# Output scatters held on GpSimd until batch 1's sorted rows are loaded

## The chip, the core and the metric

The kernel runs on one core of a Trainium2 chip. TensorE multiplies and transposes, VectorE and ScalarE move and transform tiles, GpSimd here adds constants early on and later issues the scatters, and SP issues plain DMAs. The metric is the device time of one execution in microseconds.

## What is computed

Two transformer layers over x of shape 2 x 512 x 128 (two batches of 512 tokens): attention against 77 keys, a feed-forward with low-rank experts, attention again, and at last a feed-forward that sends each token to one of 8 experts. Only the last part matters here:

```python
t = x.reshape(-1, d)                       # normalised rows
route_prob = softmax(t @ switch_w + switch_b)
routes = argmax(route_prob, axis=-1)
for e in range(8):
    h = gelu(t @ w1[e] + b1[e])            # 128 -> 512
    y = h @ w2[e] + b2[e]                  # 512 -> 128
    out = where(routes == e, y, out)
out = out * route_prob_max                 # and x + out is the result
```

## The kernel before

The last part sorts the rows by expert, each batch for itself. A batch has 4 tiles of 128 tokens, and its sorted rows fill at most 11 tiles (NSB), since each expert begins a new tile; both batches have NS = 22 tiles, 0 to 10 for batch 0 and 11 to 21 for batch 1. The way of a batch is:

- VectorE works out a slot for each row (`rank`, L809 to L823) and its probability (`prob`).
- GpSimd scatters the rows with their normalised form, probability and token number from ROW to the DRAM tensor `slots`: four indirect DMAs a batch (L514), each of which adds 16 to `rows_sent[b]`.
- SP waits for these four and loads the sorted rows back into XS in four pieces (L433): tiles 0, 1 to 2, 3 to 5 and 6 to 10 of the batch (LOADS). Each piece has its own semaphore `slots_in[b][i]`.
- For each tile t, TensorE transposes XS (L1079), ScalarE copies the expert's first weights (L621) and the transpose (L623), TensorE makes the first product (L1086), VectorE adds the bias (L846), ScalarE applies gelu (L628), TensorE makes the second product (L1097), and VectorE adds the bias (L855, YB) and scales and adds the residual into XS (L856, which signals `z_ready`). The first product of tile t stands in TensorE's list right ahead of the second product of tile t - 2.
- GpSimd scatters XS[:, t, 0:D] into the output by token number (L520), 22 indirect DMAs in the order of t, each behind `z_ready`. Its last wait is for all of them (`stored`, L523).

Each engine runs its own list of instructions in the order of one table (`schedule`). On GpSimd the four row scatters of batch 0 come first, then those of batch 1, then the 22 output scatters. TensorE waits for a piece of the load before it transposes the first tile of it (L1076), and VectorE once a piece for the token numbers (L852). No other engine waits for the output scatters, and XS has room for all 22 tiles, so no tile's place is used twice.

Of the kernel before, what the change touches and what calls it, by code (L numbers as in the profile page):

```python
# [30 lines left out]
B = 2  # L31
# [31 lines left out]
LOADS = [(0, 1), (1, 3), (3, 6), (6, NSB)]  # L63
# [127 lines left out]
def build(nc, x, ctx3, att0, att1, consts, small, rows, ffn0w, loraB, sw, w1, b1, w2, b2, empty, out):  # L191
# [9 lines left out]
    with stages:  # L201
# [3 lines left out]
        def sem(name):  # L205
            return stages.enter_context(nc.semaphore(name))
# [138 lines left out]
        slots_in = [[sem(f"slots_in{b}_{i}") for i in range(len(LOADS))] for b in range(B)]  # L345
# [61 lines left out]
        @block.sync  # L407
        def _(sp):
            xv = x.rearrange("(b t p) d -> b p t d", b=B, p=128)
            sp.dma_start(X[:, 0], xv[0]).then_inc(in_x[0], 16)  # L410
            sp.dma_start(ATT[0][:, 0:A_Q], att0[:, 0:A_Q]).then_inc(in_wk, 16)
            sp.dma_start(ATT[0][:, A_Q:], att0[:, A_Q:]).then_inc(in_att[0], 16)
            sp.dma_start(X[:, 1], xv[1]).then_inc(in_x[1], 16)
            sp.dma_start(ROWS[:, :], rows.partition_broadcast(128)).then_inc(in_rows, 16)
            sp.dma_start(W0[:, :], ffn0w).then_inc(in_w0, 16)
            for i in range(3):
                sp.dma_start(LB[32 * i:32 * i + 32, :], loraB).then_inc(in_lb, 16)
            sp.dma_start(ATT[1][:, :], att1).then_inc(in_att[1], 16)
            sp.dma_start(SW[:, :], sw).then_inc(in_moe, 16)
            sp.dma_start(B1[:, :], b1).then_inc(in_moe, 16)  # L420
            sp.dma_start(B2[:, :], b2.partition_broadcast(128)).then_inc(in_moe, 16)
            for e in range(E):
                sp.dma_start(W1[:, e * F:(e + 1) * F], w1[:, e]).then_inc(in_w1[e], 16)
                sp.dma_start(W2[:, e * NF * D:(e + 1) * NF * D], w2[:, e]).then_inc(in_w2[e], 16)
            sv = slots.rearrange("(t p) w -> p t w", p=128)
            flat = "(p t) w -> p (t w)"
            sp.dma_start(slots.rearrange(flat, p=128), empty.rearrange(flat, p=128)).then_inc(preset, 16)
            for b in range(B):

                sp.wait_ge(rows_sent[b], 16 * NQ)  # L430
                for i, (t0, t1) in enumerate(LOADS):
                    t0, t1 = b * NSB + t0, b * NSB + t1
                    sp.dma_start(XS[:, t0:t1], sv[:, t0:t1]).then_inc(slots_in[b][i], 16)  # L433

        @block.gpsimd
        def _(pool):
            counts = {}

            def finish(ins, signal):

                counts[signal.name] = counts.get(signal.name, 0) + 1
                ins.then_inc(signal, 1)
                pool.wait_ge(signal, counts[signal.name])

            finish(pool.memset(eps[:, :], EPS), zeroed)

            finish(pool.memset(KG[:, :, 0::2, GK:GP].bitcast(F32), 0.0), zeroed)
            finish(pool.memset(KG[:, :, 1::2, 0:PAD].bitcast(F32), 0.0), zeroed)
            finish(pool.memset(MR[:, :, :, :, :], 0.0), zeroed)
            finish(pool.memset(MR[:, :, :, :, 0:2], 1.0), zeroed)  # L450
            finish(pool.memset(VP[:, :, :, :, :, HALF * VC:], 0.0), zeroed)
            pool.wait_ge(in_small, 16)
            finish(pool.tensor_scalar(tau8[:, :], SMALL[:, S_TAU:S_TAU + B], RS8, None, ALU.mult), tau_ready)
            r = slice(ONES, KR)
            sel = [SMALL[r, S_SEL + i:S_SEL + i + 1] for i in range(3)]
            finish(pool.tensor_scalar(dscaled[r, :], SMALL[r, S_DEL:S_DEL + B * KEYS], RS8, None, ALU.mult), delta_part)
            finish(pool.tensor_copy(dhigh[r, :], dscaled[r, :]), delta_part)
            finish(pool.tensor_tensor(dlow[r, :], dscaled[r, :], dhigh[r, :].bitcast(F32), ALU.subtract), delta_part)

            finish(pool.tensor_scalar(dscaled[r, :], dlow[r, :], sel[1], sel[2], ALU.mult, ALU.subtract), delta_part)  # L460
            finish(pool.tensor_scalar(dlow[r, :], dhigh[r, :].bitcast(F32), sel[0], None, ALU.mult), delta_part)
            low = dlow[r, :].unsqueeze(1).to_broadcast([KR - ONES, G, B * KEYS])
            rest = dscaled[r, :].unsqueeze(1).to_broadcast([KR - ONES, G, B * KEYS])
            finish(pool.tensor_tensor(Ks[r].rearrange("p g b k -> p g (b k)"), low, rest, ALU.add), delta_ready)
            pool.wait_ge(in_con, 16)

            vm = CON[0:TW, C_VM:C_VM + NT * HALF].rearrange("p (j h) -> p j h", j=NT)
            def ones_columns(l, b):
                for half in range(2):
                    o = VP[:, l, b, :, half, 0:HALF * VC].rearrange("p j (h c) -> p j h c", c=VC)[:, :, :, DK]  # L470
                    finish(pool.tensor_copy(o, vm), ones_col)

            def moe_constants():
                tail = CON[:, C_TAIL:C_TAIL + 4 * TILES].rearrange("p (t c) -> p t c", c=4)
                finish(pool.tensor_copy(ROW[:, :, 2 * D:RW], tail), rows_set)
                finish(pool.tensor_copy(trib[:, :], CON[:, C_TRI:C_TRI + 128]), binary)
                finish(pool.memset(onesb[:, :], 1.0), binary)

            finish(pool.memset(mhalf[:, :], -0.5), powers)
            for s in steps:  # L480
                if s[0] == "ln" and s[1] == 3:
                    b = s[2]
                    pool.wait_ge(var_ready, b + 1)
                    pool.tensor_tensor(rstd[:, b], var_eps[:, b], mhalf[:, :], ALU.pow).then_inc(rstd3_ready, 1)
                if s[0] == "vp" and s[3] == 0:
                    ones_columns(s[1], s[2])
                if s == ("km", 1, 0):
                    moe_constants()
                if s[0] == "km" and s != ("km", 0, 0):
                    _, l, b = s  # L490
                    pool.wait_ge(k_split, B * l + b + 1)
                    pool.wait_ge(delta_ready, 1)
                    if l == 1:

                        pool.wait_ge(scores_ready, 2 * NT * (b + 1))
                    for odd in (0, 1):
                        finish(pool.tensor_tensor(*masked_k(b, odd), ALU.mult), kg_pool)  # L497
                elif s[0] == "xt" and s[1] < 3:

                    _, st, b = s  # L500
                    c = (R_BO0, R_WOB, R_BO1)[st]
                    if s == ("xt", 0, 0):
                        pool.wait_ge(in_rows, 16)
                    pool.wait_ge(xn_ready, (nth["xn", st, b] + 1) * NQ)
                    row = ROWS[:, c:c + D].unsqueeze(1).to_broadcast([128, NQ, D])
                    finish(pool.tensor_tensor(X[:, b], X[:, b], row, ALU.add), pre_added)  # L506
                elif s[0] == "rank":

                    b = s[1]
                    pool.wait_ge(preset, 16)  # L510
                    pool.wait_ge(slot_ready, b + 1)
                    pool.wait_ge(p_ready, b + 1)
                    for i in range(b * NQ, (b + 1) * NQ):
                        pool.indirect_dma_start(slots, bass.IndirectOffsetOnAxis(ap=slot[:, i:i + 1], axis=0), ROW[:, i], None,  # L514
                                                bounds_check=NS * 128 - 1, oob_is_err=False).then_inc(rows_sent[b], 16)
                elif s[0] == "moe" and s[1] >= 2:

                    t = s[1] - 2
                    pool.wait_ge(z_ready, t + 1)
                    pool.indirect_dma_start(out, bass.IndirectOffsetOnAxis(ap=token[:, t:t + 1], axis=0), XS[:, t, 0:D], None,  # L520
                                            bounds_check=B * S - 1, oob_is_err=False).then_inc(stored, 16)

            pool.wait_ge(stored, 16 * NS)  # L523

        @block.scalar
        def _(act):
# [7 lines left out]
            for s in steps:  # L534
                kind = s[0]
                if kind == "ln":

                    _, st, b = s
                    if st == 3:
                        continue  # L540
# [659 lines left out]
```

## Time and profile before

| | |
|---|---|
| median of 3 runs | 209.26 us (208.22 to 212.48) |
| the profiled execution | 207.62 us |
| its span | 205.7 us |
| mean granted clock of TensorE | 0.934 |
| TensorE busy | 170.5 us (83%) |
| VectorE busy | 134.2 us (65%) |
| ScalarE busy | 88.4 us (43%) |
| GpSimd busy | 59.5 us (29%) |

The span is what lies between the first and the last instruction of the profiled execution; times in rows are microseconds from its start. A busy engine is not by that alone the one that sets the time: the chain of waits tells which work ended last at each step. A granted clock of 1.00 is 2.4 GHz and 0.50 is 1.2 GHz.

### The profile page before, as it was taken

Reading aid. Unit: us, or ns where it says so; the run is one execution under the profiler, and the core shown is the slowest. Engines: PE = TensorE matmul, PEld = TensorE weight load, DVE = VectorE, ACT = ScalarE, POOL = GpSimd, SP = SyncE. Lnnn points to the kernel's source line nnn. Section 1 sums busy time; section 2 is a strip of 40 time slices with the busy share of each in tenths; the row PEclk is TensorE's granted clock in tenths of the full one; section 3 lists DMA queues with packets and bytes.
Section 4 is the critical chain, followed back from the end, with each engine's and each line's share of the span. In section 5 each row is a group of like instructions: output and inputs, shape, how many; then the busy total and the mean of one; then the engine's idle time right before and its main releaser. Section 6 shows DMA issues by size and latency. Waiting matters only on the chain.

```text
span 205.7 us, 3632 instructions
## 1 busy us (share of the span) xinstructions
PE 170.5 (83%) x1141; PEld 143.6 (70%) x1141; DVE 134.2 (65%) x388; ACT 88.4 (43%) x170; POOL 59.5 (29%) x73
## 2 busy tenths in 40 slices
PE   7556999989999967698999998952878599999960
PEld 2315888979958944574986778851868599999950
DVE  6889987589653778983347966454386266666750
ACT  2270268334542353322258163341354357677710
POOL 8992030000405160100020002054006454545551
PEclk9965599999999999999999999999679969999996
DMA  5999970000000000000000000012801560000000
GB/s 200 290 356 407 506 304 3 0 0 3 2 0 3 0 0 0 2 3 0 0 0 0 3 0 0 0 55 86 254 0 65 141 192 21 29 9 4 21 24 2
DMA packets 9218, 15.36 MB, mean 75 GB/s; under 512 B 1578, under 2 KB 6069, under 8 KB 9136
## 3 DMA queue, kind: packets, MB, share of 16 engines
q1 hardware_dynamic: 7680, 13.00, 18.3%
q0 software_dynamic: 1088, 1.60, 2.4%
q10 hardware_dynamic: 432, 0.53, 0.7%
q8 instruction: 10, 0.16, 0.3%
q14 instruction: 8, 0.07, 0.1%
HBM read 13.53 MB, written 5.44 MB: 92 GB/s over the span
## 4 chain that ended last, share of the span: by engine, by line
PE 56%; DVE 26%; issue 8%; ACT 5%; POOL 2%; DVEq 1%; ACTq 0%; another core or an unknown queue 0%; POOLq 0%
PE acc L985 12%; PE scores L1086 8%; PE acc L1097 7%; PE shared L941 5%; DVE QG L711 4%; PE scores L966 4%; PE shared L1042 4%; PE shared L1028 3%; PE shared L916 2%; PE shared L895 2%; PE shared L923 2%; DVE stats L652 2%; DVE QG L643 2%; DVE XN L670 2%; PE shared L1002 2%
## 5 line engine op out<-in xcount | busy, mean ns | idle before, releaser
L985 PE MATMUL acc<-VP,P 123*128 123x128 f32 (+1 forms) x320 | 41.8, 276 | 0.6 <-ACT P L588 0.6
L985 PEld LDWEIGHTS acc<-VP,P 123*128 123x128 f32 (+1 forms) x320 | 39.8, 191 | 2.8 <-issue 1.3
L588 ACT ACTIVATE P<-scores 123x512 f32<-123x512 f32 (+1 forms) x40 | 22.9, 595 | 27.0 <-PE scores L966 24.2
L1086 PE MATMUL scores<-XST,HT 128*128 128x128 f32 x176 | 26.3, 297 | 3.3 <-ACT XST L623 3.3
L721 DVE TENSOR_REDUCE MR<-shared 128x4 f32<-128x308 f32 x64 | 26.9, 469 | 2.2 <-PE shared L941 2.0
L520 POOL DMA_INDIRECT out<-XS,token x22 | 21.3, 969 | 20.3 <-DVE XS L856 18.3
L506 POOL TENSOR_TENSOR X<-X,ROWS 128x512 f32<-128x512 f32 x6 | 7.7, 1278 | 66.8 <-DVE XN L670 66.7
L1086 PEld LDWEIGHTS scores<-XST,HT 128*128 128x128 f32 x176 | 23.7, 209 | 4.4 <-ACT XST L623 4.3
L941 PE MATMUL shared<-KG,QG 98*128 98x308 f32 x64 | 21.3, 389 | 6.1 <-DVE QG L711 2.9
L846 DVE TENSOR_TENSOR HT<-scores,B 128x512 f32<-128x512 f32 x22 | 15.2, 691 | 16.3 <-PE scores L1086 13.1
L1097 PE MATMUL acc<-W,HT 128*128 x176 | 24.5, 286 | 0.2 <-DVE XS L856 0.2
L1097 PEld LDWEIGHTS acc<-W,HT 128*128 128x128 f32 x176 | 22.8, 203 | 0.4 <-issue 0.4
L628 ACT ACTIVATE HT<-HT 128x512 f32<-128x512 f32 x22 | 13.9, 630 | 17.9 <-DVE HT L846 10.0
L966 PE MATMUL scores<-QG,KG 102*123 102x512 f32 (+1 forms) x48 | 19.7, 458 | 1.7 <-issue 1.6
L941 PEld LDWEIGHTS shared<-KG,QG 98*128 98x128 f32 x64 | 12.7, 213 | 11.3 <-issue 5.2
L711 DVE SCALAR_TENSOR_TENSOR QG<-shared,ATT,QG 32x512 fp32r<-32x512 f32 x16 | 11.9, 745 | 6.1 <-ACT QG L575 5.8
L514 POOL DMA_INDIRECT slots<-ROW,slot x8 | 8.1, 1015 | 21.8 <-DVE ROW L789 11.4
L621 ACT ACTIVATE HT<-W 128x512 f32 x22 | 13.8, 629 | 1.2 <-issue 0.9
L575 ACT ACTIVATE QG<-shared,ATT 64x512 fp32r<-64x512 f32 x16 | 10.9, 684 | 5.4 <-PE shared L923 5.2
L580 ACT ACTIVATE QG<-shared 6x512 fp32r<-6x512 f32 x8 | 4.7, 585 | 17.7 <-PE shared L950 17.6
L966 PEld LDWEIGHTS scores<-QG,KG 102*123 102x123 f32 (+1 forms) x48 | 8.4, 191 | 3.5 <-issue 2.5
L497 POOL TENSOR_TENSOR KG<-Ks,CON 102x616 fp32r<-102x616 f32 x6 | 7.5, 1249 | 10.4 <-DVE Ks L685 10.0
(122 smaller groups left out, 248.4 us busy)
## 6 DMA issues: line engine op xcount, KB each, us to landing
W<-in_w SPq DMA_DIRECT2D x16, 256.0 KB, 8.5
slots<-in_empty SPq DMA_DIRECT2D x1, 2860.0 KB, 15.9
XS<-slots SPq DMA_DIRECT2D x2, 650.0 KB, 6.0
XS<-slots SPq DMA_DIRECT2D x2, 390.0 KB, 4.6
W<-in_ffn0w SPq DMA_DIRECT2D x1, 534.0 KB, 8.3
XS<-slots SPq DMA_DIRECT2D x2, 260.0 KB, 3.0
X<-in_x SPq DMA_DIRECT2D x2, 256.0 KB, 4.3
B<-in_b SPq DMA_DIRECT2D x1, 512.0 KB, 7.3
```

Source lines behind the costliest of these rows:

```text
L520: pool.indirect_dma_start(out, bass.IndirectOffsetOnAxis(ap=token[:, t:t + 1], axis=0), XS[:, t, 0:D], None, bounds_check=B * S - 1, oob_i ...
L588: act.activation(P[0:w, n % NP], scores[n % 2][0:w, :], ACT.Exp).then_inc(probs_ready, 1)
L621: act.activation(W1C[:, n % 2], W1[:, bass.ds(expert * F, F)], ACT.Identity).then_inc(w1_ready, 1)
L628: act.activation(HG1[:, t % NHB], HB[:, t % 2], ACT.Gelu_apprx_tanh).then_inc(gelu_ready, 1)
L711: dve.scalar_tensor_tensor(QG[64:96, b, g], bank(s)[64 * odd:64 * odd + 32, :], ATT[l][0:32, A_BQ + g:A_BQ + g + 1], QG[0:32, b, g].bitcas ...
L721: dve.tensor_reduce(MR[:, b, qt, g, 2:2 + HG], bank(s)[:, 0:GK].rearrange("p (h k) -> p h k", h=HG), AX.X, ALU.max).then_inc(max_read, 1)
L846: dve.tensor_tensor(HB[:, t % 2].rearrange("p (k n) -> p k n", k=NF), hidden[t % 2][:, :].rearrange("p (k n) -> p k n", k=NF), bias, ALU.a ...
L941: pe.matmul(bank(s)[:, 0:GK], QG[0:ONES + 2, b, g, 128 * qt:128 * qt + 128], KG[0:ONES + 2, b, g, off:off + GK], start=True, stop=True).th ...
L966: ins = pe.matmul(scores[n % 2][0:w, :], KG[:, b, g, c:c + w], QG[:, b, g], start=(i == 0), stop=(i == len(parts) - 1))
L985: ins = pe.matmul(acc[qt // 2][:, c:c + VW], P[0:w, n % NP, 128 * qt:128 * qt + 128], VP[0:w, l, b, j, half], start=(t == 0 and qt % 2 == ...
L1086: ins = pe.matmul(hidden[t % 2][:, 128 * k:128 * (k + 1)], W1C[:, t % 2, 128 * k:128 * (k + 1)], XST[:, t % 2], start=True, stop=True)
L1097: ins = pe.matmul(acc[n % 2][:, 0:D], HG1[:, n % NHB, 128 * k:128 * (k + 1)], W2[:, bass.ds(expert[n] * (NF * D) + D * k, D)], start=(k == ...
```

## The change

Ahead of the scatter of tile 0 GpSimd now waits for the four pieces of batch 1's load.

```diff
@@ -516,6 +516,9 @@
                 elif s[0] == "moe" and s[1] >= 2:
 
                     t = s[1] - 2
+                    if t == 0:
+                        for i in range(len(LOADS)):
+                            pool.wait_ge(slots_in[B - 1][i], 16)
                     pool.wait_ge(z_ready, t + 1)
                     pool.indirect_dma_start(out, bass.IndirectOffsetOnAxis(ap=token[:, t:t + 1], axis=0), XS[:, t, 0:D], None,
                                             bounds_check=B * S - 1, oob_is_err=False).then_inc(stored, 16)
```

On GpSimd, at the end of its list, with the semaphores that each instruction waits for (`slots_in1_0` to `slots_in1_3` are the four pieces of batch 1; L523 is the scatter's line in the changed file, L520 before):

```order
 L514 DMA slots<-ROW,slot 2816x260 [waits p_ready,slot_ready,preset]
 L514 DMA slots<-ROW,slot 2816x260 x3
-L520 DMA out<-XS,token 1024x128 [waits z_ready] x22
+L523 DMA out<-XS,token 1024x128 [waits slots_in1_3,slots_in1_2,z_ready,slots_in1_1,slots_in1_0]
+L523 DMA out<-XS,token 1024x128 [waits z_ready] x21
 L201 UNCONDITIONAL_BRANCH [waits stored]
```

No instruction changes its place, on this engine or another; the first of the 22 output scatters has four more waits.

## Rows read from the trace of the kernel before

**Rows 1.** Part 4 of the page: shares of the chain of waits by engine.

```profile
PE 56%; DVE 26%; issue 8%; ACT 5%; POOL 2%; DVEq 1%; ACTq 0%; another core or an unknown queue 0%; POOLq 0%
```

**Rows 2.** Chain in order of time: start us, us, what.

```profile
191.05 0.89 PE scores L1086 x8
191.94 0.89 PE acc L1097 x8
192.83 0.11 PE shared L1079
...
200.71 0.97 POOL out L520
```

**Rows 3.** Timeline of GpSimd: start us, us, engine, line, operation [idle before it]

```profile
155.18 1.04 POOL L514 DMA_INDIRECT slots<-ROW,slot  x1 [11.38 <-DVE ROW L789]
...
160.35 0.97 POOL L520 DMA_INDIRECT out<-XS,token  x1 [0.30 <-issue]
161.62 0.97 POOL L520 DMA_INDIRECT out<-XS,token  x1 [0.30 <-issue]
165.41 0.97 POOL L520 DMA_INDIRECT out<-XS,token  x1 [2.81 <-DVE XS L856]
...
171.47 0.97 POOL L520 DMA_INDIRECT out<-XS,token  x1 [1.54 <-DVE XS L856]
...
181.16 0.97 POOL L520 DMA_INDIRECT out<-XS,token  x1 [1.13 <-DVE XS L856]
...
190.66 0.97 POOL L520 DMA_INDIRECT out<-XS,token  x1 [0.93 <-DVE XS L856]
...
198.13 0.97 POOL L520 DMA_INDIRECT out<-XS,token  x1 [0.82 <-DVE XS L856]
199.41 1.00 POOL L520 DMA_INDIRECT out<-XS,token  x1 [0.30 <-issue]
200.71 0.97 POOL L520 DMA_INDIRECT out<-XS,token  x1 [0.30 <-issue]
```

**Rows 4.** The load queue's timeline: the last of batch 1's four loads.

```profile
162.97 0.49 SPq L433 DMA_DIRECT2D XS<-slots  x1
```

**Rows 5.** Part 6 of the page: issues of this kind, KB each, median us to landing.

```profile
XS<-slots SPq DMA_DIRECT2D x2, 650.0 KB, 6.0
```

**Rows 6.** Windows: PE, PEld, DVE, ACT, POOL busy, PEclk, DMA share, GB/s.

```profile
165.00:166.00 1.00, 1.00 (x7) 1.00 (x6) 0.92 (x3) 0.19 (x1) 0.59 (x1) 0.50 1.06 293
...
168.00:169.00 1.00, 1.00 (x9) 1.00 (x9) 0.17 (x1) 0.98 (x3) 0.22 (x2) 0.81 0.17 47
169.00:170.00 1.00, 1.00 (x11) 1.00 (x10) 0.69 (x1) 0.24 (x2) 0.94 (x1) 1.00 0.00 0
```

**Rows 7.** TensorE: line L1079's waits (us, times), then its timeline.

```profile
  DMA XS<-slots: 8.1, 2
...
164.19 1.40 PE L1086 MATMUL scores<-XST,HT 128*128 128x128 f32 x8 [2.12 <-ACT XST L623]
...
173.48 0.27 PE L1079 MATMUL shared<-CON,XS 128*128 128x128 f32 x1
```

**Rows 8.** Timeline of VectorE, columns as for GpSimd.

```profile
157.70 0.69 DVE L846 TENSOR_TENSOR HT<-scores,B 128x512 f32<-128x512 f32 x1 [0.63 <-ACT HT L628]
...
161.69 0.69 DVE L846 TENSOR_TENSOR HT<-scores,B 128x512 f32<-128x512 f32 x1 [2.65 <-PE scores L1086]
...
164.26 0.35 DVE L856 SCALAR_TENSOR_TENSOR XS<-YB,XS 128x128 f32<-128x128 f32 x1
165.09 0.69 DVE L846 TENSOR_TENSOR HT<-scores,B 128x512 f32<-128x512 f32 x1 [0.47 <-issue]
...
172.22 0.35 DVE L856 SCALAR_TENSOR_TENSOR XS<-YB,XS 128x128 f32<-128x128 f32 x1
173.04 0.69 DVE L846 TENSOR_TENSOR HT<-scores,B 128x512 f32<-128x512 f32 x1 [0.46 <-PE scores L1086]
```

**Rows 9.** Line L856 as a whole: ns min/median/max, first and last start.

```profile
L856 DVE SCALAR_TENSOR_TENSOR XS<-YB,XS x22: 350/352/353, 156.7 to 199.2; 128x128 f32<-128x128 f32 x22
```

## The prediction

> **What bounds the kernel now.** I read the shares of the chain of waits first, then the chain in order of time at its end, then the timelines of the four engines and of the load queue through the last 50 us. By the shares, TensorE carries 56% of the path and GpSimd 2% [rows 1]. In the stretch that the change touches, the path is TensorE's: it is one tile after another there, first product 0.89 us, second product 0.89 us, a transpose 0.11 us, which is 1.90 us a tile. Only behind the last product does the chain leave TensorE, for VectorE's last additions and then GpSimd, whose last three scatters start at 198.13, 199.41 and 200.71 [rows 2, 3]. So GpSimd counts at the very end only. What the reader is to see: a scatter before that end is late for nobody, because the kernel has no wait on `stored` but GpSimd's own at the end, and XS[:, t] is neither loaded nor written again after the scatter of tile t.
>
> The profiled execution took 207.62 us, with a span of 205.7 us, so 1.9 us lie around the span. The median of the three runs shown is 209.26 us. I make the sum as a difference on the span and add it to the median.
>
> **What the change adds.** Four waits on constants in GpSimd's queue ahead of the scatter of tile 0, and nothing else. They are queue instructions without data: I put them at nothing; what separates two scatters that wait for nothing, 0.30 us [rows 3], bounds one of them from above, and all four lie under the hold or within the slack below.
>
> *How long is the hold?* Of batch 1's four loads SP issues the last and largest (tiles 17 to 21, 650 KB) at 162.97 [rows 4]; such a load lands 6.0 us after its issue [rows 5]. That puts the release at R = 162.97 + 6.0 = 169.0 us. The DMA share agrees: 1.06 from 165 to 166, 0.17 from 168 to 169, and 0.00 after [rows 6]. Before, tile 0's scatter ran at 160.35 right behind the four row scatters of batch 1, so the hold is real. It moves the scatters of tiles 0 to 4, the first five of the queue, behind R.
>
> *What queues up behind it?* All 22 output scatters stand behind the waiting one, and nothing else does: batch 1's row scatters stand ahead of it in the queue and are the work on which the loads depend, so there is no circle. The first scatter starts about 0.8 us after its release, as tile 2's did (its VectorE operation ends at 164.26 + 0.35 = 164.61, the scatter starts at 165.41). Back to back the scatters start 1.29 us apart: 155.18 to 161.62 holds five intervals (four row scatters, then tiles 0 and 1), 1.29 each, and 198.13 to 200.71 two, 1.29 each [rows 3, 8]. Tile k is then scattered at 169.8 + 1.29 k, as long as that is later than before. Before, they came 1.90 apart. Tile 5: 176.3 against 171.47. Tile 10: 182.7 against 181.16. Tile 15: 189.2 against 190.66. The lag of 1.5 us at tile 10 shrinks by 1.90 - 1.29 = 0.61 a tile, so it is gone at tile 13, eight tiles before the end. If it were not, the last scatter could start at 169.8 + 21 x 1.29 = 196.9; it waits for its tile and starts at 200.71 as before. **Slack 3.8 us, cost 0.**
>
> *What leaves the load window?* The DMA work of the scatters that started before R, five of them, three at 160.35, 161.62 and 165.41. If batch 1's loads get faster by that, nobody gains: over all 22 transposes TensorE's waits for a load are two records of the first one, the matmul's and its weight load's, 8.1 us together. Tile 11, the first of batch 1, is transposed at 173.48 without such a wait [rows 7]; even the last load is there 4.5 us before it. Gain 0. The bound is zero on both sides unless something else hangs on the scatters, which the rivals price.
>
> **A rule that speaks against the change.** The backlog makes GpSimd denser: 0.97 us of issuing in each 1.29 instead of in each 1.90, from 169.8 to about 187 us. VectorE's last operation of a tile reads two SBUF tensors, and it already runs into a scatter now: the one at 172.22 lies within the scatter of 171.47 to 172.44, and takes 0.35 us like the others. Its 22 instances span 350 to 353 ns, overlapped or not [rows 3, 8, 9]. So I charge nothing.
>
> The Trainium skill, page "SBUF — State Buffer", section "SBUF: two separate sides", says that VectorE and GpSimd share a pair of ports under an exclusive lock, and that a VectorE operation with two SBUF inputs against a GpSimd operation that reads SBUF leaves the second one fully blocked. By that page the scatter issue would hold such an operation up; the 353 ns maximum in this trace does not agree for this pair.
>
> **The sum.** Waits 0, backlog 0 (3.8 us of slack), loads 0, port 0: span 205.7, median 209.3 us.
>
> **Rivals.**
> *1. No change in time* (the forecast), 0.80, 209.3 us.
>
> *2. The early scatters disturb the other engines, and holding them gives that back.* There is something to explain. VectorE's bias operation of tile 4 starts at 161.69, 3.99 us after the one at 157.70, and the next at 165.09, 3.40 us later [rows 8]. Against a period of 1.90 that is 2.1 + 1.5 = 3.6 us lost. TensorE sits idle for 2.12 us until 164.19 [rows 7], and its granted clock is then 0.50 (1.2 GHz) from 165 to 166 and back at 1.00 at 169 [rows 6]; VectorE's bias operations take 7.95 us from 165.09 to 173.04, four tiles, against 7.6, another 0.35. For it: the scatters of 160.35 and 161.62 lie inside. Against it: tile 4's operation was due at 157.70 + 1.90 = 159.6, before the first output scatter started, so the first part has another cause; and the same scatters at the same density do no harm from 198 us on. If only the second part goes, 1.5 + 0.35: 209.26 - 1.9 = 207.4 us. If all of it goes, 3.95: 205.3 us. Chance 0.12, of which a third for all of it; where the stall comes differently in every execution, this moves the median either way by as much.
>
> *3. GpSimd becomes the bound at the end: slower.* The place is the scatter queue behind R. It decides from R + 0.8 + 21 x 1.29 > 200.71, that is from R = 172.8 on, or at R = 169.0 from a spacing of (200.71 - 169.8) / 21 = 1.47 us instead of 1.29. Each microsecond of R beyond it costs one. Over 2% needs R = 177.0 or a spacing of 1.67. Against it: both loads of this size took 6.0 us as a median, and the spacing is measured. For it: thirteen scatters in a row are not in the trace, six are. With a spacing of 1.6 us: 200.71 becomes 203.4, and the time 212.0 us. Chance 0.05.
>
> *4. The dense scatters hold VectorE up after all: slower.* VectorE works 0.69 + 0.35 us in its two longest operations of a tile [rows 8]; with the third, the addition of YB on half the columns of the first and so at most 0.35, that is 1.39 us in each 1.90, so it decides once the hindrance exceeds some 0.5 us a tile; a full scatter of 0.97 would cost 0.46 on each of the nine tiles that pass between 169.8 and 187 us, 4.1 us: 213.4 us. Against it stand the 353 ns. Chance 0.03.
>
> **The numbers.** The forecast is 209.3 us. The three runs of before lie from 1.0 below to 3.2 above their median, so a median of the changed kernel may lie a microsecond or two off with no cause in the change. Low end: the smaller gain of rival 2 (207.4) less about that 1.0, 206.5. High end: the middle plus two thirds of the upper scatter, 211.5; that leaves rivals 3 and 4 and the larger case of rival 2 outside, with the tails about 2 in 10. Over 2% (4.2 us, about what a measurement of this kernel can tell from no change) faster needs all of rival 2 and a little luck: 0.05. Over 2% slower: rival 4, a bad case of rival 3, or a median drawn from the upper end of such runs: 0.06. The rest is 0.89.
>
> **What would show it.** Right: GpSimd's first output scatter starts at about 169.8 and the following ones 1.28 to 1.30 apart up to about tile 13, then 1.90 apart; the last starts at the same distance from the end of the span as now, 205.7 - 200.7 = 5.0 us; TensorE's tiles keep 1.90; L856 keeps 0.35. Wrong in a step: a first scatter after 173 (the load estimate), a spacing over 1.47 (the catch-up), L856 or L846 longer (the port), or a span whose stretch from 157 to 169 us is shorter by 2 us or more (rival 2). The forecast falls if the stall near 160 us goes with the scatters and does not come back when they do.

## The result, and the profile after

| | before | changed |
|---|---|---|
| median | 209.24 us (6 runs, 208.22 to 212.48) | 215.42 us (6 runs, 213.34 to 215.91) |
| the profiled execution | 207.62 us | 214.13 us |
| its span | 205.7 us | 212.2 us |

The changed kernel took 1.027 times as long, with a 95% interval of 1.0227 to 1.0313. The forecast was 209.3 us, no change. It stands wrong for this pair. In the same comparison in later runs, on three chips, the ratio lay between 0.9987 and 1.0015, and the kernel before took 204.8 us on each of the five chips met in later runs. (The record does not name the chip that ran the pair, so it may have been a sixth chip or one of the five at another time.) So there are two things to explain, and the document keeps them apart: the pair of the record, and what the change does in the later runs.

The page of the changed kernel, busy times, then the slices of TensorE and its clock, and the chain's shares by engine. (Lines of the changed file stand three higher than those of before: L849 is the bias operation, L1089 the first product, L523 the output scatter.)

```profile
PE 173.3 (82%) x1141; PEld 146.2 (69%) x1141; DVE 134.6 (63%) x388; ACT 88.7 (42%) x170; POOL 59.6 (28%) x73
...
PE   7745999989999976779999998636997991799960
...
PEclk9996799999999999999999999975569999699996
...
PE 50%; DVE 28%; issue 8%; another core or an unknown queue 4%; ACT 4%; POOL 2%; DVEq 2%; ACTq 0%; POOLq 0%
```

Busy times have hardly moved, GpSimd still has 2% of the path, and 4% of it are now put down to "an unknown queue", where [rows 1] had 0%. TensorE has a hole near four fifths of the span. GpSimd's timeline shows the hold and what follows:

```profile
160.34 0.97 POOL L514 DMA_INDIRECT slots<-ROW,slot  x1 [0.30 <-issue]
170.97 1.04 POOL L523 DMA_INDIRECT out<-XS,token  x1 [9.66 <-DMA XS<-slots]
172.31 0.97 POOL L523 DMA_INDIRECT out<-XS,token  x1 [0.30 <-issue]
...
179.96 0.97 POOL L523 DMA_INDIRECT out<-XS,token  x1 [0.30 <-issue]
182.56 0.97 POOL L523 DMA_INDIRECT out<-XS,token  x1 [1.64 <-DVE XS L859]
...
207.22 0.97 POOL L523 DMA_INDIRECT out<-XS,token  x1 [0.30 <-issue]
```

The first output scatter comes at 170.97 and not at 160.35 [rows 3]; eight of them start 1.27 to 1.34 us apart; and at the ninth it is GpSimd that waits for VectorE. So the queue of scatters had caught up by tile 8, and was not what made the kernel later. VectorE's bias operations were late instead:

```profile
158.97 0.69 DVE L849 TENSOR_TENSOR HT<-scores,B 128x512 f32<-128x512 f32 x1 [0.64 <-ACT HT L631]
...
162.28 0.69 DVE L849 TENSOR_TENSOR HT<-scores,B 128x512 f32<-128x512 f32 x1 [1.97 <-remote]
...
171.63 0.69 DVE L849 TENSOR_TENSOR HT<-scores,B 128x512 f32<-128x512 f32 x1 [0.46 <-PE scores L1089]
...
176.81 0.69 DVE L849 TENSOR_TENSOR HT<-scores,B 128x512 f32<-128x512 f32 x1 [3.74 <-remote]
183.34 0.69 DVE L849 TENSOR_TENSOR HT<-scores,B 128x512 f32<-128x512 f32 x1 [1.57 <-remote]
185.59 0.69 DVE L849 TENSOR_TENSOR HT<-scores,B 128x512 f32<-128x512 f32 x1 [0.82 <-issue]
```

The steps of tiles 9 to 10 to 11 are 5.2 and 6.5 us, where 1.90 is the rule. Two more operations that wait for TensorE alone start late there: VectorE's addition behind the second product of tile 8, and ScalarE's copy of the transpose of tile 12.

```profile
181.09 0.29 DVE L858 TENSOR_TENSOR YB<-acc,B 128x128 f32<-128x128 f32 x1 [3.59 <-remote]
```

```profile
181.01 0.28 ACT L626 ACTIVATE XST<-shared 128x128 f32<-128x128 f32 x1 [2.16 <-remote]
```

TensorE's own rows in that stretch (L1100 is the second product, L1082 the transpose; those of 173.07 and 173.97 belong to tiles 8 and 12):

```profile
170.28 1.06 PE L1089 MATMUL scores<-XST,HT 128*128 128x128 f32 x8
...
172.18 1.06 PE L1089 MATMUL scores<-XST,HT 128*128 128x128 f32 x8
173.07 1.06 PE L1100 MATMUL acc<-W,HT 128*128 x8
173.97 0.27 PE L1082 MATMUL shared<-CON,XS 128*128 128x128 f32 x1
174.08 1.06 PE L1089 MATMUL scores<-XST,HT 128*128 128x128 f32 x8
...
181.35 2.04 PE L1089 MATMUL scores<-XST,HT 128*128 128x128 f32 x8 [5.21 <-ACT XST L626]
```

The product of tile 10 stands in the trace from 172.18 to 173.24, and VectorE, which waits for nothing else, begins on it at 176.81: 3.6 us later, and "remote" means that no recorded work ended then. Further down TensorE's list the lateness is larger: the second product of tile 8 ends in the record at 174.13 and is taken up at 181.09 (7.0 us), the transpose of tile 12 at 174.24 and 181.01 (6.8 us), tile 11's first product at 175.14 and 183.34 (8.2 us). ScalarE sees it as VectorE does, so the cause does not lie in VectorE alone. Tile 9's product, still undisturbed, ended at 170.28 + 1.06 = 171.34 and was taken up at 171.63, 0.3 us later. Either TensorE's work was really late and its record is not (the ends of matmuls are modelled), or its signals were; these rows do not tell which. I call it the late signals. TensorE itself then idles 5.21 us, until ScalarE's late copy for tile 12 is there, and its granted clock falls from 1.00 to 0.50. Windows of 2 us, columns as in [rows 6]:

```profile
174.00:176.00 2.00, 2.00 (x20) 1.90 (x18) 0.00 (x0) 0.00 (x0) 1.52 (x2) 1.00 0.02 1
176.00:178.00 2.00, 0.14 (x2) 0.00 (x0) 0.69 (x1) 0.47 (x1) 1.56 (x2) 1.00 0.08 19
178.00:180.00 2.00, 0.00 (x0) 0.00 (x0) 0.00 (x0) 0.79 (x2) 1.39 (x3) 1.00 0.10 33
180.00:182.00 2.00, 0.65 (x3) 0.66 (x4) 0.64 (x2) 0.28 (x1) 0.93 (x1) 0.85 0.14 46
182.00:184.00 2.00, 2.00 (x11) 2.00 (x11) 0.66 (x1) 0.00 (x0) 0.97 (x1) 0.50 0.00 0
```

DMA is nearly idle there, and GpSimd alone keeps its pace. The kernel before has the same thing on a smaller scale. The first product of tile 4 and the second of tile 2 end in the record at 159.11 and 160.00, and VectorE takes them up at 161.69 [rows 8] and 163.94, 2.6 and 3.9 us later; ScalarE's copy at 163.86 is 3.8 us behind its transpose.

```profile
157.95 1.16 PE L1086 MATMUL scores<-XST,HT 128*128 128x128 f32 x8 [0.68 <-ACT XST L623]
158.94 1.06 PE L1097 MATMUL acc<-W,HT 128*128 x8
```

```profile
163.94 0.29 DVE L855 TENSOR_TENSOR YB<-acc,B 128x128 f32<-128x128 f32 x1 [1.55 <-remote]
```

**Where the 6.5 us of span went.** From the bias operation of tile 3 to that of tile 21 the trace of before has 157.70 to 195.77, 38.1 us, the changed one 158.97 to 202.28, 43.3 us, and behind that both have 9.9 us. So 5.2 us lie in the tiles 3 to 21, and 1.3 us had been lost before tile 3, ahead of anything that the change touches. An undisturbed trace (below) has 34.0 us for the same 18 steps: before lost 4.0 us in the record pair, the changed kernel 9.3, each with the lower clock behind the late signals.

The 5.2 us are a difference of two things. From tile 3 to tile 9 the kernel before takes 157.70 to 173.04, 15.3 us [rows 8], the changed one 158.97 to 171.63, 12.7 us, and the undisturbed trace 11.3: the stall near 160 us has shrunk from 4.0 to 1.4 us, a gain of 2.7. From tile 9 to tile 12 the changed kernel takes 171.63 to 185.59, 14.0 us, where the other two take 6.0: a loss of 7.9 behind the hold. From there on all three are alike. Each figure is from one execution.

### The profile page after: what moved, and what is told of

It reads as the page before. It is cut to its first block, busy times and chain, and to the rows that moved or that the text cites. A ratio compares the mean times of both kernels' runs of the same rounds, so it can differ in the third digit from the quotient of the medians.

```text
span 212.2 us, 3634 instructions
## 1 busy us (share of the span) xinstructions
PE 173.3 (82%) x1141; PEld 146.2 (69%) x1141; DVE 134.6 (63%) x388; ACT 88.7 (42%) x170; POOL 59.6 (28%) x73
## 4 chain that ended last, share of the span: by engine, by line
PE 50%; DVE 28%; issue 8%; another core or an unknown queue 4%; ACT 4%; POOL 2%; DVEq 2%; ACTq 0%; POOLq 0%
PE acc L988 11%; PE scores L1089 6%; PE shared L944 5%; PE acc L1100 4%; DVE QG L714 4%; PE shared L1045 4%; PE scores L969 4%; DVE HT L849 2%; PE shared L1031 2%; PE shared L898 2%; PE shared L919 2%; PE shared L926 2%; DVE stats L655 2%; PE shared L1018 2%
## 5 line engine op out<-in xcount | busy, mean ns | idle before, releaser
L1089 PE MATMUL scores<-XST,HT 128*128 128x128 f32 x176 | 27.9, 309 | 7.3 <-ACT XST L626 7.1
L1089 PEld LDWEIGHTS scores<-XST,HT 128*128 128x128 f32 x176 | 25.2, 221 | 8.8 <-ACT XST L626 8.4
L523 POOL DMA_INDIRECT out<-XS,token x22 | 21.4, 972 | 25.5 <-DVE XS L859 13.1
L849 DVE TENSOR_TENSOR HT<-scores,B 128x512 f32<-128x512 f32 x22 | 15.2, 692 | 19.8 <-PE scores L1089 9.4
L944 PE MATMUL shared<-KG,QG 98*128 98x308 f32 x64 | 20.8, 381 | 7.7 <-DVE QG L714 7.2
L1100 PE MATMUL acc<-W,HT 128*128 x176 | 24.8, 288 | 0.2 <-DVE XS L859 0.2
L1100 PEld LDWEIGHTS acc<-W,HT 128*128 128x128 f32 x176 | 23.0, 205 | 0.4 <-issue 0.4
```

The source lines that it names most:

```text
L849: dve.tensor_tensor(HB[:, t % 2].rearrange("p (k n) -> p k n", k=NF), hidden[t % 2][:, :].rearrange("p (k n) -> p k n", k=NF), bias, ALU.a ...
L944: pe.matmul(bank(s)[:, 0:GK], QG[0:ONES + 2, b, g, 128 * qt:128 * qt + 128], KG[0:ONES + 2, b, g, off:off + GK], start=True, stop=True).th ...
L1089: ins = pe.matmul(hidden[t % 2][:, 128 * k:128 * (k + 1)], W1C[:, t % 2, 128 * k:128 * (k + 1)], XST[:, t % 2], start=True, stop=True)
L1100: ins = pe.matmul(acc[n % 2][:, 0:D], HG1[:, n % NHB, 128 * k:128 * (k + 1)], W2[:, bass.ds(expert[n] * (NF * D) + D * k, D)], start=(k == ...
```

## The experiments

Each was compared with the kernel before, run beside it on the same chip. "This chip" is below the chip of the run in question. I began with the nearest theory: a dense run of scatters (1.28 us apart) makes TensorE's signals late. For it spoke that all work of TensorE that was taken up late, in both traces, ends in the record while such a run is going on: at 159.11 and 160.00 in the run of scatters that start from 155.18 to 161.62 [rows 3], and in the changed kernel at 160.38 (tile 4, taken up 1.9 us late) in that from 156.45 to 160.34, and from 173.24 to 175.14 in that from 170.97 to 179.96. Against it spoke that batch 0's four row scatters, from 135.47 on in the kernel before and from 135.70 on in the changed one, are as close and have no such wait behind them, though TensorE is busy only half of the time there. The sizes go with the length of the run: 1.4 us lost with four scatters in a row, 4.0 with six, 7.9 with eight. Three stretches in two executions are no proof of it.

**Scatters spaced by a memset, hold kept.**

```diff
                                             bounds_check=B * S - 1, oob_is_err=False).then_inc(stored, 16)
+                    finish(pool.memset(gap[:, 0:256], 0.0), gapped)
```

> The changed kernel (hold kept), with one 256-column memset on GpSimd behind each output scatter, so that the scatters behind the hold come about 1.6 us apart and not 1.28. Theory A (a dense run of scatters, 0.97 us of issuing in each 1.28, holds TensorE's completions back): TensorE's stall from 173 to 184 us goes or shrinks to under 3 us, 209 to 212 us. Theory B (the hold itself or the freed load window does it, whatever comes after): 214 to 216 us, with the stall at the same place. Theory C (VectorE and GpSimd block each other on SBUF, and more GpSimd work makes it worse): over 216 us.

It took 222.54 us beside 204.77, 1.0858 (1.0813 to 1.0903). The memset with its wait spaced the scatters 2.09 us apart and not 1.6, and that is over the 1.90 of a tile: the queue ran from the first scatter at 171.78 to the last at 215.81 = 171.78 + 21 x 2.097 without ever waiting for a tile. TensorE had no late signal. The run was mis-sized for its question and shows rival 3 of the prediction instead, GpSimd as the bound. The kernel before at 204.8 us was the first sign that these runs differ from the record pair in something other than the kernel.

**Lag of five tiles, no catching up while TensorE works.**

```diff
-                    pool.wait_ge(z_ready, t + 1)
+                    pool.wait_ge(z_ready, min(t + 6, NS))
```

> The changed kernel, with scatter t waiting for tile t + 5 and not for tile t: the same hold, the same lag of some five tiles for all of the run, but no catching up while TensorE works; scatters 1.90 us apart there and the last six in a row after it. Theory A: no stall after the hold, TensorE's last product ends at about 199 to 201 us of the span, and only the tail is longer, by about 5 x 1.29 = 6.4 us: 214 to 217 us with TensorE done early. Theory B: TensorE stalls as in the changed kernel, last product at 205, and the tail on top: 220 us and more.

211.51 us beside 204.77, 1.0311 (1.0258 to 1.0363). The tail of GpSimd's timeline:

```profile
196.33 0.97 POOL L523 DMA_INDIRECT out<-XS,token  x1 [0.81 <-DVE XS L859]
197.60 1.00 POOL L523 DMA_INDIRECT out<-XS,token  x1 [0.30 <-issue]
...
205.29 0.97 POOL L523 DMA_INDIRECT out<-XS,token  x1 [0.30 <-issue]
```

TensorE began its last product at 195.78. Eight scatters in a row then start up to 205.29, 9.0 us from the first to the last (six were expected); the kernel before has three such at its end, so five more, 6.4 us, against 6.7 measured. The tail is sized as expected; on density it says nothing, since TensorE was undisturbed on this chip in every variant.

**Two bursts of eight, no wait for the loads.**

```diff
-                    pool.wait_ge(z_ready, t + 1)
+                    pool.wait_ge(z_ready, 8 * (t // 8 + 1) if t < 16 else t + 1)
```

> The kernel before, without any wait for the loads, but its scatters let go in two bursts of eight: tiles 0 to 7 when tile 7 is ready, tiles 8 to 15 when tile 15 is ready. Theory A: TensorE stalls from about 3 us after the start of each burst until its end, each costing 6 us or so: 215 to 222 us. Theory B: nothing waits for these scatters, 208 to 211 us.

211.96 us beside 204.77, 1.0378 (1.0331 to 1.0426), inside the expected range and for another reason. GpSimd's timeline:

```profile
181.15 0.97 POOL L520 DMA_INDIRECT out<-XS,token  x1 [0.30 <-issue]
187.58 0.97 POOL L520 DMA_INDIRECT out<-XS,token  x1 [5.46 <-DVE XS L856]
...
204.19 0.97 POOL L520 DMA_INDIRECT out<-XS,token  x1 [0.30 <-issue]
```

Eight scatters in a row to 181.15 and fourteen from 187.58, and VectorE's bias operations stood 1.6 to 2.3 us apart through both, as in any undisturbed trace. The 7 us are the queue's: 187.58 + 13 x 1.28 = 204.2, where tile 21, with its bias operation at 192.69, would have let the last scatter go at 197.6. A time inside the range would have passed for a proof here; the rows refute it. A dense run alone, on a chip where the kernel before takes 204.8 us, does not make the signals late.

**Batch 1's row scatters spaced, no hold.**

```diff
                                             ROW[:, i], None, ...).then_inc(rows_sent[b], 16)
+                        if b == 1:
+                            finish(pool.memset(gap[:, 0:640], 0.0), gapped)
```

(and the same behind the first output scatter).

> The kernel before, with a 640-column memset (about 0.65 us) behind each of batch 1's four row scatters and behind the first output scatter, so that this run of six comes about 1.9 us apart and not 1.28; batch 1's load then starts some 2.6 us later and still lands before tile 11 is wanted. Theory A: the stall of 3.6 us in VectorE's bias operations near 160 us goes, and the lower clock behind it: 205 to 207 us. Theories B and C, and a stall with another cause: 209 us within 1 us, and the stall is where it was.

204.66 us beside 204.77, 0.9995 (0.9973 to 1.0017). There was no stall near 160 us on this chip to take away. The row scatters came 2.4 us apart; the backlog behind them was worked off in a dense run from 169.12 to 183.11, again harmlessly.

**The changed kernel and the kernel before, unaltered, and a shorter hold.** The third waits for the first load piece only.

```diff
-                        for i in range(len(LOADS)):
-                            pool.wait_ge(slots_in[B - 1][i], 16)
+                        pool.wait_ge(slots_in[B - 1][0], 16)
```

> The changed kernel once more, unaltered, beside the kernel before. The four runs so far, with dense scatter runs in three of them, showed no TensorE stall at all, and the kernel before took 204.8 us there. Theory A' (the stall needs the dense run and something that differs from chip to chip): on a chip where the kernel before takes about 205 us, the changed kernel takes 204 to 206 us too, with scatters 1.28 us apart after the hold and no stall; on a chip where the kernel before takes about 209 us, 213 to 216 us with a stall. Theory B (the hold costs its 5 to 6 us on every chip): 210 to 212 us beside 205.

> The kernel before, unaltered, for its profile on this chip. Theory A': where it takes about 205 us, VectorE's bias operations of tiles 3 to 8 come 1.8 to 2.0 us apart with no gap of 3.4 or 4.0 us near 160 us, and the granted clock does not fall to 0.50 there; the 3.6 us of that gap are then most of the difference between 209 and 205 us. Theory D (the chips differ elsewhere, in transfers or clock): the gap is there, and the difference lies in another stretch.

> The changed kernel with the hold reduced to the first of batch 1's four load pieces, which lands some 4 us earlier, so that fewer scatters run 1.28 us apart behind it. Theory A': same as the kernel before where there is no stall; where there is one, between the kernel before and the changed kernel, 2 to 4 us over before. Theory B: half of the changed kernel's loss, on any chip.

On another chip: changed 205.39 beside 204.80, 1.0015 (0.9983 to 1.0046); before against itself 0.9968 (0.9941 to 0.9995); shorter hold 1.0013 (0.9989 to 1.0038). The spread of before against itself, 0.3%, is what such a comparison can be off by. Here the change costs nothing. First the changed kernel's bias operations of tiles 3, 12 and 21, then the same three of the kernel before:

```profile
159.59 0.69 DVE L849 TENSOR_TENSOR HT<-scores,B 128x512 f32<-128x512 f32 x1 [0.62 <-ACT HT L631]
...
176.92 0.69 DVE L849 TENSOR_TENSOR HT<-scores,B 128x512 f32<-128x512 f32 x1 [0.82 <-PE scores L1089]
...
193.62 0.69 DVE L849 TENSOR_TENSOR HT<-scores,B 128x512 f32<-128x512 f32 x1 [0.22 <-PE scores L1089]
```

```profile
160.15 0.69 DVE L846 TENSOR_TENSOR HT<-scores,B 128x512 f32<-128x512 f32 x1 [0.62 <-ACT HT L628]
...
177.49 0.69 DVE L846 TENSOR_TENSOR HT<-scores,B 128x512 f32<-128x512 f32 x1 [0.81 <-PE scores L1086]
...
194.18 0.69 DVE L846 TENSOR_TENSOR HT<-scores,B 128x512 f32<-128x512 f32 x1 [0.21 <-PE scores L1086]
```

Both take 34.03 us from tile 3 to tile 21: the hold and the dense run change nothing in TensorE's pace on this chip. In the kernel before tiles 3 to 8 come 1.80 to 2.04 us apart and the granted clock is 1.00 from 158 to 170 us, as theory A' expected; the 4.0 us that the record's trace lost there are most of the 4.4 us between 209.2 and 204.8. And the changed kernel's scatters:

```profile
171.55 0.97 POOL L523 DMA_INDIRECT out<-XS,token  x1 [9.61 <-DMA XS<-slots]
...
181.77 1.08 POOL L523 DMA_INDIRECT out<-XS,token  x1 [0.30 <-issue]
...
198.57 0.97 POOL L523 DMA_INDIRECT out<-XS,token  x1 [0.30 <-issue]
```

They run back to back from the first to the last: 171.55 + 21 x 1.287 = 198.57. In the kernel before the last scatter starts 4.94 us after tile 21's bias operation (194.18 and 199.12), here 4.95 us (193.62 and 198.57). The queue catches the last tile just in time. In three further traces of the changed kernel (below) every scatter starts right behind the one before, and the last starts 5.0 to 5.5 us after tile 21's bias operation (5.49, 5.10 and 5.02 us), so the queue is late by 0.1 to 0.6 us. The slack that the prediction put at 3.8 us is zero or slightly less where no signal is late.

**Again on the same chip, later.** The changed kernel, and the lag of five tiles.

> The changed kernel again, unaltered, for the chip that this call meets. Two levels have been seen: the kernel before near 209 us with a stall of TensorE's signals near 160 us, and near 205 us without one on two other chips. Theory A': beside a kernel before near 209 us this takes 213 to 216 us, with TensorE's signals late by 2 us and more inside the dense scatter run; beside one near 205 us it takes 204 to 206 us. Theory E (the 2.7% was one sitting of the first chip and is tied to nothing in the kernel): 0 to 1% apart beside either level.

> The hold kept, the scatters let go one tile time apart (scatter t waits for tile t + 5), as in the run with lag 5 before. Theory A': beside a kernel before near 209 us TensorE has at most a short stall behind the hold and ends its last product 4 us or more earlier than in the changed kernel; beside one near 205 us it gives 210 to 212 us again, all of it the six scatters behind the last tile. Theory B: beside 209 us the same stall as in the changed kernel.

205.21 us beside 204.81, 1.0012 (0.9989 to 1.0036), and 211.13 us, 1.0276 (1.0108 to 1.0444, with two runs of it). Both answer to the branch of an undisturbed chip, so neither could tell theory A' from B or E.

**Row scatters apart, with the hold.** The changed kernel with `finish(pool.memset(gap[:, :], 0.0), gapped)`, 256 columns, behind each of batch 1's row scatters.

> The changed kernel with its hold and the dense run behind it, and with a 256-column memset behind each of batch 1's four row scatters, so that those come 2.1 us apart and not 1.28. Within one profile it has a spaced stretch (157 to 166 us) and a dense one (from about 174 us). Theory A' beside a kernel before near 209 us: TensorE's tiles stay 1.9 us apart in the first stretch and stall in the second only. Theory F (TensorE stalls by itself on such a chip, at times that have nothing to do with GpSimd): stalls in both or in the first only. Beside a kernel before near 205 us neither stretch has a stall; the hold then ends some 2.4 us later than in the changed kernel, when the queue of scatters was already just about as late as the last tile, and the last scatter comes some 2 to 3 us later: 207 to 208 us.

On a third chip: 207.88 us beside 204.79, 1.0146 (0.9969 to 1.0324, with two runs of it, 206.36 and 209.41). The first and the last output scatter:

```profile
175.62 0.97 POOL L527 DMA_INDIRECT out<-XS,token  x1 [10.02 <-DVE XS L863]
...
202.50 0.97 POOL L527 DMA_INDIRECT out<-XS,token  x1 [0.30 <-issue]
```

No late signals again, so theories A' and F were not told apart. But the first scatter comes 4.07 us later than the 171.55 above, with a stage that is 1.05 us later (tile 21 at 194.67 against 193.62), so the hold is 3.0 us longer, and the queue pays for it: 175.62 + 21 x 1.28 = 202.50, where tile 21, with its bias operation at 194.67, would have let the last scatter go at 194.67 + 4.94 = 199.6. That is 2.9 us, and the two runs' middle lies 3.1 us over the kernel before. The interval does not exclude zero; the two trace rows carry the reading.

**A DRAM to DRAM copy during the dense run,** with the hold and without it.

```diff
+            sp.dma_start(copy.rearrange(flat, p=128), empty.rearrange(flat, p=128)).then_inc(copied, 16)
+            sp.wait_ge(copied, 16)
```

> The changed kernel with a DRAM to DRAM copy of 2.86 MB behind batch 1's loads on SP, which nobody but SP waits for; it takes 16 us in the trace and so fills the DMA engines from about 170 to 186 us, while the held scatters run 1.28 us apart. Theory G (TensorE's signals are late where dense scatters meet DMA traffic; on the first chip the traffic was not this kernel's own): TensorE's tiles fall out of the 1.90 us step by 2 us and more, 208 us and more. Theory H (own traffic plays no part): TensorE keeps 1.90; scatters may land later, 205 to 207 us.

> The kernel before with the same copy, as the counterpart without a dense run. Theory G: no stall or a shorter one, 1 us or less over the kernel before. Theory H: the same as the other, within 1 us.

On a fourth chip: 205.25 us beside 204.81, 0.9999 (0.9956 to 1.0041), and 204.84 us, 1.0010 (0.9975 to 1.0044). Windows of the first:

```profile
168.00:170.00 2.00, 2.00 (x20) 2.00 (x19) 1.50 (x5) 1.51 (x4) 0.00 (x0) 1.00 1.56 573
...
174.00:176.00 2.00, 2.00 (x20) 2.00 (x19) 1.34 (x4) 1.52 (x4) 1.67 (x2) 1.00 0.96 366
176.00:178.00 2.00, 2.00 (x20) 2.00 (x20) 1.23 (x3) 1.20 (x3) 1.39 (x3) 1.00 0.19 42
```

The copy kept the DMA engines busy at 350 GB/s and more until about 176 us, shorter than expected, and overlapped the first four held scatters (from 171.5 on). TensorE stayed full. On this chip the kernel's own traffic beside a dense run does not make the signals late either.

**Two last repeats of the changed kernel.**

> The changed kernel unaltered, once more, for the chip that this call meets; the kernel before has taken 204.8 us on the three chips met so far. If the kernel before is near 209 us here, the changed one takes 213 to 216 us and shows late signals of TensorE in the dense run (theory A'). If it is near 205 us, the changed one is within 1% of it.

> The changed kernel unaltered on whatever chip this call meets. Beside a kernel before near 209 us: 213 to 216 us and late signals of TensorE in the dense run. Beside one near 205 us: within 1%.

204.93 us beside 204.77, 0.9987 (0.9956 to 1.0018), on the third chip, and 205.03 us beside 204.80, 1.0009 (0.9975 to 1.0043), on a fifth. The level of 209 us was not met again, and without it none of these runs could test what made the signals late.

## Why the prediction was wrong, point by point

- **The hold** was forecast to end at 169.0 and the first scatter to start at 169.8. It started at 170.97, which is 1.2 us later; the whole stage runs 1.3 us later in this execution. Right.
- **The spacing** of 1.29 us: right in every run (1.28 as a mean, up to 22 in a row). The backlog lasted through eight scatters and not thirteen, because TensorE's late tiles let it catch up. In the later runs of the unaltered changed kernel, without them, it lasted to the end, through all 22.
- **The cost of the backlog, 0 because of 3.8 us of slack.** This term was mis-sized, though it did not make the result. The slack was read from a trace whose tiles were themselves 4.0 us late, and 3.8 - 4.0 leaves nothing. Undisturbed, the scatters run back to back to the end, and the last is 0.0 to 0.6 us late. The cost is still within 0.15% of zero in the four repeats, but by luck, not by slack: in the run with the row scatters apart 3.0 us more of hold cost 2.9 us, where a slack of 3.8 would have covered them.
- **The loads and the waits:** no engine but the held GpSimd waited for batch 1's loads in any of the changed kernel's traces, and the four waits cost nothing that shows. Right.
- **The port:** VectorE's operation with two SBUF inputs took at most 354 ns in the changed trace. (The one at 172.22 that the prediction reads as inside a scatter only begins inside it and ends 0.13 us behind it; both have their usual length.) On the undisturbed chip its maximum is 419 ns, once in 22, where it starts 0.10 us ahead of a scatter:

```profile
177.84 0.42 DVE L859 SCALAR_TENSOR_TENSOR XS<-YB,XS 128x128 f32<-128x128 f32 x1
```

```profile
177.94 0.97 POOL L523 DMA_INDIRECT out<-XS,token  x1 [0.30 <-issue]
```

  In the same trace the scatter of 1.08 us at 181.77 starts 0.11 us behind such an operation, which took 0.35. The Trainium skill, page "SBUF — State Buffer", section "SBUF: two separate sides", has whichever of the two starts first take the ports for its whole length and the other blocked, where the GpSimd operation reads SBUF. The prediction took a scatter's issue for one, which the section does not say. If it is one, an overlap would cost VectorE up to 0.97 us, an estimate by that page and the scatter's row; the trace does not agree, with 0.07 us at most.
- **The step that failed** is the term that the sum holds at nothing: that only GpSimd's own end hangs on the scatters, so that behind the hold "TensorE's tiles keep 1.90". They did not: from tile 9 to tile 11 the steps were 5.2 and 6.5 us, and from tile 9 to tile 12 the changed kernel lost 7.9 us. The cause of that stays open. Rival 2 came nearest, and its own sign was even seen: the tiles 3 to 9 took 2.7 us less in the changed trace, and those up to 169 us 2.5 us less, more than the 2 us that the prediction names as a sign of it. It saw the late tile 4, dismissed a link with the scatters by two arguments, and priced only a gain. Neither argument excludes a link. One was that tile 4 was due at 159.6, before the first output scatter; but the row scatters had been running 1.28 us apart from 155.18, with the output scatters right behind them. The other was that the same density does no harm from 198 us on; but there TensorE had almost nothing left to do, since its last product had begun by then:

```profile
197.59 1.15 PE L1097 MATMUL acc<-W,HT 128*128 x8 [0.18 <-DVE XS L856]
```

  But the gain was overrun by a stall of a size that the prediction gave to nothing. The late signals were there in both traces of the record pair and cost more in the changed kernel, 9.3 us against 4.0. That the longer dense run, eight scatters where TensorE works all the time, made them larger is not shown. No case of the prediction had a loss of this kind: its two slower rivals put it on GpSimd's queue and on VectorE's ports.

What the runs put in its place: in the record pair the 6.5 us of span are 7.9 us of late signals of TensorE behind the hold, less 2.7 us that the stall near 160 us shrank by, and 1.3 us that were lost ahead of tile 3. In the later runs, on five chips, the dense run, up to 22 scatters long and once beside extra traffic, disturbs nothing, and on the three of them that ran the changed kernel unaltered the change costs between -0.13% and +0.15%, which is no more than the comparison can be off by. Take the 4.0 us from the 207.62 us of the kernel before in the record pair, and 203.6 remain; take 9.3 and 1.3 us from the 214.13 of the changed one, and 203.5 remain. The unaltered kernels' profiled executions elsewhere took 203.6 to 206.0 us. So in these two traces the late signals, with the lower clock behind them, account for what sets the record pair apart.

**What stays open.** The cause of the 2.7%. That the late signals come from the dense run is argued from their place in two traces, not shown: the level of 209 us was not met again, so neither the spaced nor the bursting variant ran where it could have told. Theory F, that TensorE stalls there whatever GpSimd does, stands untested as well; what it would have to explain is that all six runs of the changed kernel in the record pair, 213.34 us and more, lie above all six of the kernel before, 212.48 us and less. Whether it is the chip, the time of the runs or something outside this core that makes TensorE's signals sensitive is open too. Nor is it known whether the work or the signal was late.

## What to carry to other kernels

A slack that is read from one trace is only as good as the pace of that trace: where an engine shows unexplained late steps, work the slack out a second time with those steps at their usual length. A queue that issues at 1.28 us behind a producer of 1.90 catches up only 0.62 us a tile, so a delay of 10 us takes 16 tiles to forget, and one late order for 22 scatters goes straight to the end. And where two kernels differ by 3% and the difference sits in rows that the profile calls "remote", compare them again, on a second chip if possible, before believing either sign.

## What the runs showed that was not expected

- In the record pair VectorE and ScalarE take up TensorE's work 2.6 to 3.9 us late (kernel before) and 1.9 to 8.2 us late (changed kernel), with matmul records that look undisturbed; the profile names "remote" as the releaser (7.3 us in three waits of L849). None of the 14 traces of later runs, on five chips, has such a row.
- The kernel before takes 209.2 us in the record pair's runs and 204.8 us in the later runs on each of five chips.
- A 256-column memset of 0.33 us between two scatters, with a wait for it, adds 0.8 us to their distance (1.28 to 2.09), since the next scatter begins 0.79 us after the memset's end.
- Where VectorE's operation with two SBUF inputs starts about 0.1 us ahead of a scatter, one of the two can be some 0.1 us longer than usual: 0.42 us in place of 0.35, or a scatter of 1.08 in place of 0.97.
